# Two MLP layers of a gated transformer block: first product by pairs of tiles in split float32r products, norm moved to ScalarE, loads and statistics one step earlier

## The reference

```
h = shift_token(x)                         # half of the features come from the row before
mu = h.mean(-1); var = h.var(-1)
h = (h - mu) / sqrt(var + 1e-05) * lg + lb
h = h @ w1 + b1                            # 128 -> 2 x 341
a, g = split(h)
h = a * gelu(g)
x = x + h @ w2 + b2                        # 341 -> 128
```

## Time and profile before

| what | value |
|---|---|
| median of 3 runs | 1178.89 us (1174.58 to 1181.09) |
| the profiled execution's own time | 1174.67 us |
| its span in the trace | 1172.9 us |
| PE busy | 1088.3 us, 93% of the span |
| DVE busy | 989.7 us, 84% |
| ACT busy | 924.7 us, 79% |
| POOL busy | 730.6 us, 62% |

### The profile page before, as it was taken

The page is one execution under the profiler, slowest core; times in us unless marked ns, Lnnn a source line. Parts: engine busy times, 40 slices in busy tenths (PEclk is TensorE's granted clock), DMA queues, the critical chain, the costliest instruction groups (busy, mean ns, idle before and its releaser), DMA issues.

```text
span 1172.9 us, 33608 instructions
## 1 busy us (share of the span) xinstructions
PE 1088.3 (93%) x11412; PEld 922.1 (79%) x11412; DVE 989.7 (84%) x2339; ACT 924.7 (79%) x2616; POOL 730.6 (62%) x1090
## 2 busy tenths in 40 slices
PE   6899976999999989979999999989989997999996
PEld 3777754888888879967888888888867776799996
DVE  4799968999889858878899889768889997599988
ACT  4898866999999975559999999865578886876672
POOL 4799937777777744437777777634589994444431
PEclk9999989999999999999999999999999999999999
DMA  6000000111111112111112310111000000000000
GB/s 201 22 2 1 2 15 17 29 29 29 29 28 24 24 27 65 34 23 23 30 29 47 83 28 19 31 25 28 17 2 2 3 1 2 6 13 14 15 15 16
DMA packets 62408, 30.79 MB, mean 26 GB/s; under 512 B 46197, under 2 KB 56481, under 8 KB 62242
## 3 DMA queue, kind: packets, MB, share of 16 engines
q1 hardware_dynamic: 59474, 27.15, 9.7%
q10 hardware_dynamic: 2768, 1.51, 0.5%
HBM read 9.77 MB, written 2.10 MB: 10 GB/s over the span
## 4 chain that ended last, share of the span: by engine, by line
PE 63%; DVE 14%; ACT 9%; issue 8%; POOL 4%; DMA 0%; DVEq 0%; ACTq 0%; POOLq 0%
PE m_ps_y L1512 7%; PE a_ps_b L1030 5%; PE a_ps_t L1041 5%; PE a_ps_s L936 5%; PE a_ps_a L963 5%; PE a_ps_t L1005 4%; PE a_ps_qk L920 4%; DVE x_e L692 3%; PE f_ps_y L1299 3%; PE f_ps_g L1310 3%; PE a_ps_qk L921 2%; PE a_ps_qk L922 2%; PE f_ps_a L1317 2%; PE a_ps_s L977 2%; PE m_ps_h L1499 2%
## 5 line engine op out<-in xcount | busy, mean ns | idle before, releaser
L1108 ACT ACTIVATE a_e<-a_ps_s,a_stat 128x128 f32<-128x128 f32 x512 | 226.6, 477 | 3.1 <-DVE a_stat L1177 3.1
L1239 POOL TENSOR_TENSOR a_rot<-a_rot 128x512 f32<-128x512 f32 x64 | 82.7, 1293 | 136.1 <-DVE a_rot L1131 136.1
L1233 POOL TENSOR_TENSOR a_e<-a_e,a_stat 128x1024 f32<-128x1024 f32 x64 | 121.4, 1897 | 5.8 <-DVE a_stat L1156 5.8
L1108 ACT ACTIVATION_READ_ACCUMULATOR a_e<-a_ps_s,a_stat 128x1 f32 x512 | 115.7, 226 | 0.0
L1346 ACT ACTIVATE f_gl<-f_ps_g,vec 128x128 f32<-128x128 f32 (+1 forms) x192 | 55.8, 361 | 58.7 <-PE f_ps_g L1310 58.7
L1227 POOL TENSOR_TENSOR a_rot<-a_rot 128x512 f32<-128x512 f32 x64 | 81.6, 1275 | 18.2 <-DVE a_rot L1131 18.2
L1129 DVE TENSOR_TENSOR a_rot<-a_ps_qk,a_rtab 128x512 f32<-128x512 f32 x128 | 86.9, 679 | 0.0
L1131 DVE TENSOR_TENSOR a_rot<-a_ps_qk,a_rtab 128x512 f32<-128x512 f32 x128 | 86.8, 678 | 0.0
L741 DVE TENSOR_REDUCE x_stat<-x_ps_s 128x16 f32<-128x1024 f32 x64 | 77.1, 1205 | 11.4 <-PE x_ps_s L547 11.3
L1173 DVE TENSOR_REDUCE a_stat<-a_ps_s 128x8 f32<-128x1024 f32 x64 | 77.8, 1215 | 4.7 <-PE a_ps_s L936 4.5
L1166 DVE TENSOR_REDUCE a_stat<-a_sq 128x16 f32<-128x1024 f32 x64 | 78.0, 1218 | 3.5 <-ACT a_sq L1115 2.1
...
## 6 DMA issues: line engine op xcount, KB each, us to landing
...
```

The source lines that it names most:

```text
L1108: act.activation(self.e[n % 2][:, P * i:P * i + P], ps_s[:, P * i:P * i + P], ACT.Exp, bias=stat[:, 24 + i:25 + i], scale=stat[:, root:roo ...
L1233: p.tensor_tensor(e3, e3, self.stat[n % UNROLL][:, 16:24].unsqueeze(2).broadcast_to([P, 8, P]), ALU.mult)\
L1239: p.tensor_tensor(r, r, self.rot2[:, INNER:], ALU.add).then_inc(self.s_n, 1)
```

## The change

- The norm moves from DVE to ACT: POOL makes a third small operation, the shift -mean x rstd (`rstd_shift`), and ACT applies scale and shift (`affine`). Statistics and root have four slots instead of two.
- Loads are issued at step n - 1 instead of n, and the statistics and the root are at step n + 1 instead of n + 2. The norm stays at step n + 3.
- Two tiles of a sequence are transposed into one PSUM bank. ACT writes the rounded part of both at once (`hTh`, 256 columns, with lg), and DVE the rest (`hTl`).
- w1 is split into a rounded part `w1h` (ACT) and a rest `w1l` (POOL), once per layer, at step -6. These and `hTh` and `act` lie in the memory of `kT[0]` and `vall[0]`, which the first cross stage has finished with.
- `ps_g` and `ps_a` are made for a pair of tiles: six chunks of three float32r matmuls with 256 columns. `ps_g` is at the even step behind the pair, `ps_a` one step later. Gelu and `act` work on 256 columns.
- `ps_y` moves from step n + 7 to n + 8, to the end of PE's program for the step.
- lb is no longer added to `hT`: at step 3 of each layer PE makes lb @ w1 with six matmuls of one column, and DVE adds this to b1.

The core of the diff:

```diff
+PREP = -6
...
+    def rstd_shift(self, g, k, t):
+
+        g.wait_ge(self.s_st, 2 * k + 2)
+        after(g, self.s_nm, k - self.slots + 1)
+        g.tensor_scalar(t[:, 8:9], t[:, 7:8], 1e-5, None, ALU.add).then_inc(self.s_rs, 1)
+        g.wait_ge(self.s_rs, 3 * k + 1)
+        g.tensor_tensor(t[:, 9:10], t[:, 8:9], self.g.neg_half, ALU.pow).then_inc(self.s_rs, 1)
+        g.wait_ge(self.s_rs, 3 * k + 2)
+        g.tensor_scalar(t[:, 10:11], t[:, 6:7], t[:, 9:10], -1.0, ALU.mult, ALU.mult).then_inc(self.s_rs, 1)
+
+    def affine(self, act, k, t, dst, src):
+        act.wait_ge(self.s_rs, 3 * k + 3)
+        act.activation(dst, src, ACT.Identity, bias=t[:, 10:11], scale=t[:, 9:10]).then_inc(self.s_nm, 1)
...
+        self.ln = Norm(g, "f_ln", UNROLL)
+        self.h, self.hn = self.many("h", UNROLL, D), self.many("hn", 2, D)
+        keys, values = g.kT[0], g.vall[0]
+        self.w1h, self.w1l = keys[:, 0:6 * P], keys[:, 6 * P:12 * P]
+        self.hTh, self.hTl = [keys[:, 12 * P + S * i:12 * P + S * i + S] for i in range(2)], self.many("hTl", 2, S, F32R)
+        self.st = self.many("st", UNROLL, 16)
+        self.gl, self.yo = self.many("gl", 2, 3 * S), self.many("yo", 2, D)
+        self.act = [values[:, 3 * S * i:3 * S * i + 3 * S] for i in range(2)]
...
     def sync(self, sp, l, s):
-        if s == 0 and not l:
+        if s == -1 and not l:
             sp.wait_ge(self.s_z, 2)
-        n = s
+        n = s + 1
         if 0 <= n < T:
             k = T * l + n
             sp.wait_ge(self.local.s_yc, k + 1)
             after(sp, self.ln.s_nm, k - UNROLL + 1)
...
+    def product(self, pe, dst, c, b, signal):
+
+        at = slice(P * c, P * c + P)
+        pe.matmul(dst, self.w1h[:, at], self.hTh[b % 2][:, :], start=True, stop=False)
+        pe.matmul(dst, self.w1l[:, at], self.hTh[b % 2][:, :], start=False, stop=False)
+        pe.matmul(dst, self.w1h[:, at], self.hTl[b % 2][:, :], start=False, stop=True).then_inc(signal, 1)
...
+        if s == 3:
             pe.wait_ge(g.s_mw, g.n_mw * (l + 1))
+            self.take(pe, l, "x")
+            for i, lo in enumerate((0, HID)):
+                for c, w in enumerate(HCH):
+                    m = pe.matmul(ps_x[1][0:w, S + 3 * i + c:S + 3 * i + c + 1], g.mw1[:, lo + P * c:lo + P * c + w], g.vec[:, 1:2],
+                                  start=True, stop=True)
+            m.then_inc(self.s_bp, 1)
...
+            pe.transpose(ps_x[b % 2][:, P * u:P * u + P], self.hn[u][:, :], g.ident).then_inc(self.s_t, 1)
+        n = s - 5
+        if 0 <= n < T and n % 2:
+            b, q = n // 2, T // 2 * l + n // 2
+            pe.wait_ge(self.s_hc, q + 1)
+            pe.wait_ge(self.s_hl, q + 1)
+            after(pe, self.s_gl, 3 * q)
+            if b == 0:
+                pe.wait_ge(self.s_wh, 2 * l + 2)
+                pe.wait_ge(self.s_wl, 2 * l + 2)
+                pe.wait_ge(self.s_z, 8)
+                self.take(pe, l, "g")
+            for c in range(3):
+                self.product(pe, ps_g[:, S * c:S * c + S], c, b, self.s_g)
+        n = s - 6
+        if 0 <= n < T and n % 2:
+            b, q = n // 2, T // 2 * l + n // 2
+            after(pe, self.s_ac, 3 * q)
+            if b == 0:
+                self.take(pe, l, "a")
+            for c in range(3):
+                self.product(pe, ps_a[:, S * c:S * c + S], 3 + c, b, self.s_a)
...
+        if s == PREP:
             act.wait_ge(g.s_mw, g.n_mw * (l + 1))
+            act.wait_ge(self.cross.s_up, T)
+            after(act, self.s_a, 3 * T // 2 * l)
+            act.activation(self.w1h[:, 0:HID], g.mw1[:, HID:2 * HID], ACT.Copy).then_inc(self.s_wh, 1)
+            act.activation(self.w1h[:, 3 * P:3 * P + HID], g.mw1[:, 0:HID], ACT.Copy).then_inc(self.s_wh, 1)
...
+            act.activation(self.hTh[b % 2][:, :], ps_x[b % 2][:, 0:S], ACT.Copy, scale=g.vec[:, 0:1]).then_inc(self.s_hc, 1)
+        n = s - 3
+        if 0 <= n < T:
+            after(act, self.s_t, T * l + n - 1)
+            self.ln.affine(act, T * l + n, self.st[n % UNROLL], self.hn[n % 2][:, :], self.h[n % UNROLL][:, :])
...
+                act.wait_ge(self.s_g, 3 * q + max(c, 1) + 1)
+                act.activation(self.gl[b % 2][0:w, S * c:S * c + S], ps_g[0:w, S * c:S * c + S], ACT.Gelu,
...
+            for rows, c in ((slice(0, P), slice(0, 2)), (slice(0, HCH[2]), slice(2, 3))):
+                v.tensor_tensor(bias[rows, :, c], more[rows, :, c], bias[rows, :, c], ALU.add).then_inc(self.s_bf, 1)
...
+            v.scalar_tensor_tensor(out=self.hTl[b % 2][:, :], in0=ps_x[b % 2][:, 0:S], scalar=g.vec[:, 0:1], in1=self.hTh[b % 2][:, :],
+                                   op0=ALU.mult, op1=ALU.subtract).then_inc(self.s_hl, 1)
...
+                at = slice(S * c, S * c + S)
+                v.wait_ge(self.s_gl, 3 * q + c + 1)
+                v.wait_ge(self.s_a, 3 * q + max(c, 1) + 1)
+                v.scalar_tensor_tensor(out=self.act[b % 2][0:w, at], in0=ps_a[0:w, at], scalar=g.vec[0:w, 2 + c:3 + c],
+                                       in1=self.gl[b % 2][0:w, at], op0=ALU.add, op1=ALU.mult).then_inc(self.s_ac, 1)
...
-        n = s - 3
-        if 0 <= n < T:
-            after(v, self.s_t, T * l + n - 1)
-            self.ln.norm(v, T * l + n, self.st[n % 2], self.hn[n % 2][:, :], self.h[n % UNROLL][:, :])
...
+        n = s - 1
+        if 0 <= n < T:
+            k = T * l + n
+            v.wait_ge(self.s_d[n % UNROLL], landed(k))
+            self.ln.stats(v, k, self.st[n % UNROLL], self.h[n % UNROLL][:, :])
...
+    def pads(self, p):
+
+        p.wait_ge(self.cross.s_up, T)
         for t in self.act:
-            p.memset(t[64:P, 2 * P:3 * P], 1.0).then_inc(self.s_z, 1)
-        p.wait_ge(self.s_z, 4)
+            p.memset(t[:, 2 * S:3 * S], 1.0).then_inc(self.s_z, 1)
+        for t in (self.w1h, self.w1l):
+            for i in range(2):
+                p.memset(t[:, 3 * P * i + HID:3 * P * i + 3 * P].bitcast(F32), 0.0).then_inc(self.s_z, 1)
...
+        if s == PREP:
+            if not l:
+                self.pads(p)
+            after(p, self.s_a, 3 * T // 2 * l)
+            for i, (at, lo) in enumerate(((0, HID), (3 * P, 0))):
+                p.wait_ge(self.s_wh, 2 * l + i + 1)
+                p.tensor_tensor(self.w1l[:, at:at + HID], self.g.mw1[:, lo:lo + HID], self.w1h[:, at:at + HID], ALU.subtract)\
+                    .then_inc(self.s_wl, 1)
+        n = s - 1
+        if 0 <= n < T:
+            self.ln.rstd_shift(p, T * l + n, self.st[n % UNROLL])
```

More of the change, by code:

```diff
@@ L252, with __init__ @@
 class Norm:
-    def __init__(self, g, name):
-        self.g = g
+    def __init__(self, g, name, slots=2):
+        self.g, self.slots = g, slots
         self.s_st, self.s_rs, self.s_nm = (g.sem(f"{name}_{i}") for i in ("stats", "rstd", "norm"))
     def stats(self, v, k, t, src):
-        after(v, self.s_nm, k - 1)
+        after(v, self.s_nm, k - self.slots + 1)
         v.bn_stats(t[:, 0:6], src).then_inc(self.s_st, 1)
@@ L1298, in tensor @@
                 w += c == 2
-                m = pe.matmul(ps_y[u][:, 0:D], self.act[u][0:w, P * c:P * c + P], g.mw2[0:w, D * c:D * c + D],
+                at = S * c + P * u
+                m = pe.matmul(ps_y[u][:, 0:D], self.act[b % 2][0:w, at:at + P], g.mw2[0:w, D * c:D * c + D],
                               start=(c == 0), stop=(c == 2))
             m.then_inc(self.s_y, 1)
-        n = s - 5
-        if 0 <= n < T:
-            k, u = T * l + n, n % 2
-            pe.wait_ge(self.s_hc, k + 1)
-            after(pe, self.s_gl, 3 * (k - 1))
-            if n == 0:
-                self.take(pe, l, "g")
-            for c, w in enumerate(HCH):
-                m = pe.matmul(ps_g[u][0:w, P * c:P * c + P], g.mw1[:, HID + P * c:HID + P * c + w], self.hT[u][:, :],
-                              start=True, stop=True)
-            m.then_inc(self.s_g, 1)
-            after(pe, self.s_ac, 3 * (k - 1))
-            if n == 0:
-                self.take(pe, l, "a")
-            for c, w in enumerate(HCH):
-                m = pe.matmul(ps_a[u][0:w, P * c:P * c + P], g.mw1[:, P * c:P * c + w], self.hT[u][:, :],
-                              start=True, stop=True)
-            m.then_inc(self.s_a, 1)
     def scalar(self, act, l, s):
@@ L1332, in scalar @@
         n = s - 4
-        if 0 <= n < T:
-            k, u = T * l + n, n % 2
-            act.wait_ge(self.s_t, k + 1)
-            after(act, self.s_g, k - 1)
-            after(act, self.s_a, k - 1)
-            act.activation(self.hT[u][:, :], ps_x[u][:, 0:P], ACT.Identity, bias=g.vec[:, 1:2], scale=g.vec[:, 0:1])\
-                .then_inc(self.s_hc, 1)
-        n = s - 5
-        if 0 <= n < T:
-            k, u = T * l + n, n % 2
-            act.wait_ge(self.s_g, k + 1)
-            after(act, self.s_ac, 3 * (k - 1))
+        if 0 <= n < T and n % 2:
+            k, b, q = T * l + n, n // 2, T // 2 * l + n // 2
+            act.wait_ge(self.s_t, k + 1)
+            after(act, self.s_a, 3 * (q - 1))
```

(19 more changed lines are left out.)

72 lines of the change are left out of this document (30 added, 42 removed).

## The result

The changed kernel takes 1180.7 us (median of 20 runs, 1174.96 to 1183.73), against 1176.99 us of the kernel before on the same chip. The ratio is 1.0024, with an interval of 1.0013 to 1.0035: a quarter of a per cent slower, within the 0.5% that I had called no change. I had forecast 1169.2 us and a chance of 0.64 for faster, so the case that I had given most to was wrong. The profiled execution has a span of 1173.2 us and is the fastest of the 20; its gap of 0.3 us to the span before is smaller than the 3.7 us between the medians.

What follows compares the result with a forecast made beforehand. It took PE to bound the first MLP, DVE the second, and SP's DMA queue both afterwards. Terms -3.4 - 8.7 + 2.4 = -9.7 us on 1174.67 gave 1165.0, so a median of 1169.2; range 1155 to 1183.

Steps and rivals of the forecast that it cites:

- the case that I had given most to: Whole kernel: faster than before, chance 0.64, with 1169.2 us forecast.
- What bounds it, PE, DVE: MLP stages: PE bounds the first, DVE's loop the second; after the change PE 1.82, DVE 1.72 us a step.
- rival 3: PE in the MLPs: weight loads not hidden behind 256 columns, 2.51 us a step, 1191.6 us; chance 0.08.
- SP's queue as the new bound: Load DMAs in both MLPs: the same five per pair set the pace, 2.1 us a step.
- Rival 1: Both MLPs: SP's queue doesn't bind, PE paces at 1.82 to 1.85 us a step, 1154 us; chance 0.12.
- The second MLP: Term for its 28 steps: 2.1 us each instead of 2.41, -8.7 us.
- The first: Term for the first MLP: earlier and faster loads and an earlier end, together -3.4 us.
- What is added: Local stages and MLP step 3: ACT's rounding 0.6, POOL 0.2, bias 0.4; 1.2 us a layer, 2.4 in all.
- Rival 2: No measurable change: SP's queue at 2.30 us a tile or a tight load loop, 1179.7 us; chance 0.22.
- the range of 8 in 10: Whole kernel's time: from 1155 us, near the PE-paced case, to 1183, past the no-change case.

Runs made afterwards that it cites:

- e12: e6 with POOL's copy two steps ahead of the statistics instead of one, in eight slots: 1173.15 us.
- e9: Changed kernel with the changes of e1, e2 and e12, and DVE's bias addition at step 5 instead of 3: 1160.84 us.
- e1: Changed kernel with POOL's w1 subtractions moved behind the softmax multiplication, one in each of two steps, and its memsets spread: 1173.87 us.
- e2: Changed kernel with POOL's three small operations for root and shift moved behind the softmax multiplication: 1180.55 us.
- e6: Changed kernel with POOL copying the 64 unshifted columns in SBUF and the 127-row DMA cut into 112 and 15 rows: 1185.65 us.
- e7: Changed kernel with POOL copying the 64 unshifted columns in SBUF, 127 rows uncut, and eight slots instead of four: 1187.60 us.

## Why the prediction was wrong, step by step

**What bounds it, PE, DVE: right.** PE's free step 1.85 us (1.82 forecast), products 0.12 us apart (0.115), weight loads hidden, so rival 3 is out. `act` 1.26 and `hTl` 0.40 apart (1.18 and 0.39).

**SP's queue as the new bound: right in the first MLP**, 2.01 us a tile in quiet stretches (2.1 taken, 2.04 read), 2.06 a step over the second MLP. Rival 1 is out in this kernel; e12 shows what it would have taken. The experiments add why an issue grows beside 127 rows. But the 2.06 of the second MLP is in part luck: it is a mean of 14 pairs of steps, six near PE's own 3.7 us, three at the queue's 4.05, three of 3.98 to 4.87 beside the experts' weights, where POOL, with root, shift and a subtraction of 1.00 us a step, had no pause from 798.3 to 809.4, and two of 4.9 beside the first work of cross 1. e9, with the queue relieved, needs 57.05 us for these 28 steps, only 0.6 less; the rest of its 3.4 us in the table lies outside them, most of it (2.3) ahead of the first `ps_y`.

**The second MLP: right.** -8.7 us forecast, 93.3 to 84.6 measured, -8.6. **The first: nearly.** -3.4 forecast, -2.4 between the score products; these contain part of the local stage's longer drain. The queue's 3.69 us issue beside ACT's weight loads is in it, as I had allowed: the last load of the first MLP is issued at 495.48 us, and was at 494.99.

**The step that failed is "What is added".** I took 1.2 us a layer: 0.6 for ACT's rounding, 0.2 for POOL, 0.4 for the bias. ACT's part fits (e1 leaves 0.64 and 0.61). POOL's was not: "if POOL is late [...] up to 2 us, I take 0.2". It was late with certainty, since its wait for ACT stands ahead of the one multiplication that PE waits for. I had named the rotated tiles as what would wait; it was the exponentials. I had seen POOL's free time as a sum and not asked on which side of L1248 it lies. That cost 1.7 and 1.8 us (e1), not 0.2. And root and shift, one step earlier and so ahead of L1248 in the drain of local 0, stood at nothing in my sum; they cost 1.7 us there (e2). In all the local stages lost 4.7 and 3.2 us in the profile, 7.9 together where I took 2.4 and called 5 the other end. With e1 and e2 in, the loss is 2.1 and 1.3 (table), and the kernel comes to 1171.95, near the forecast. Also not in my sum: the clock, which fell behind such a pause in 10 of the 18 preparation steps of the nine profiles and made 2.4 us into 4.0.

**Not in the sum at all: 3.6 us behind the second MLP.** The cross stage takes 1.9 us longer at its start (1.4 to 1.9 in the variants of the table); its longest step there, 7.3 us, has PE waiting 1.28 us for ACT's `x_e` and 1.07 for DVE's. A part is only moved: since `ps_y` lies one step later, two of them (851.12 and 858.95) fall behind the first `s` of cross 1, where it was one (854.29). No experiment isolates the rest. The 1.7 us in the experts lie in code that didn't change, where the clock drops a second time; e6 and e7 take 192.0 us from there to the end, as the kernel before does. The kernel before, then the changed one (granted clock third from the end):

```profile
1011.00:1015.00 4.00, 4.00 (x30) 3.57 (x29) 0.65 (x5) 4.00 (x10) 1.92 (x5) 1.00 0.02 4
```

```profile
1011.00:1015.00 4.00, 4.00 (x23) 3.62 (x23) 0.00 (x0) 3.43 (x8) 0.85 (x3) 0.69 0.01 2
```

Added up in the profiles: the MLPs gained 1.0 us less than forecast, the local stages lost 5.5 more, and 3.6 came behind them, which makes the -9.7 of the forecast the measured +0.3. The medians add 3.4 us, half of it the clock by the count in e2. The forecast's 1169.2 also stood on the median of three runs of the kernel before, 1178.89; that of twenty is 1.9 us lower.

Rival 2 (no measurable change) had the right result by the wrong way: it had the MLPs gain little, and they gained 11 us. That 1180.7 lies inside the range of 8 in 10 is owed to this rival's share of it, so it is luck too.

What stays open: 2.6 to 3.6 us of e1's 8.9, which neither its two steps (3.5) nor the clock (1.8 by the profiles, 2.8 by whole executions) account for, and of which the intervals allow 2.5; what the bias products cost; and the 1.9 us at the cross stage's start.
